# Attention's result added to the residual by VectorE instead of by GpSimd

## The chip, the cores and the metric

The kernel runs on all 8 cores of one Trainium2 chip. Each core computes one of the batch's eight sequences, with all weights of its own, and the cores exchange nothing. The time is the device time of the slowest core in microseconds (us). Engines are called as the profile calls them: PE is TensorE (matrix products), PEld its weight loads, DVE is VectorE, ACT is ScalarE, POOL is GpSimd, SP is SyncE, which here only issues DMAs.

## The reference

x has 8 sequences of 2048 tokens with 1024 features. One layer is computed, first attention, then an FFN, each behind a layer norm and each added to its input:

```python
x = x + _L0_attn_ref(_layernorm(x, axis=-1), W_query, W_key, W_value)
x = x + _L0_ffn_ref(_layernorm(x, axis=-1), w1, conv_w, conv_b, w2)
```

Attention is causal, with 16 heads of 64 features and no projection behind it: softmax(q k / 8) v goes straight into the residual. In the FFN the weights are rounded to -1, 0 or 1 times a scale that is their mean absolute value, the activations are rounded to 8 bits with a scale per token, and between the two products stand a depthwise convolution of width 3 over the tokens and SiLU.

## The kernel before, in words

**Stages.** The program has a stretch for the first norm, the values and the first queries and keys (to about 131 us), attention (131 to about 535 us), a turn between the two (the last quarter of x1 goes to DRAM and comes back tile by tile) and the FFN (from about 574 us). `attention_over` (L298) lets every engine wait until attention is over.

**Attention.** Heads go in 8 pairs (`hp`), queries in 4 tiles of 512 (`t`), keys in chunks of 128. One pair has 4 + 8 + 12 + 16 = 40 units (`unit_of`, L35); a unit is the scores of both heads of the pair for 512 queries and 128 keys. Every engine's program runs over the same slots, one per unit, and what is done in which slot is written out by hand:
- PE (L733): in each slot the scores of the unit into psS (two buffers), in four of ten slots half a projection of the next pair's queries or keys, and then the products with the values, `context(u)` (L690), of units some slots back. They sum up in psPV, of which there is one for both heads. So the first product of a tile waits for v_epi, that is, until the tile before it has been read. The units on the diagonal wait for g_mask.
- ACT (L926): the exponential of each unit, psS to PT.
- DVE (L1200): in slot 3 of ten the cast of the next pair's queries, in slot 8 that of its keys, some small operations that bound the exponent (`norm_max`, `norm_product`, `place_bias`), the weights' steps (`weight_step`, L1131), and at slots 7, 15, 27 and 43 of a pair (the last is slot 3 of the next) `normalize_ctx` (L1109), for tiles 0 to 3.
- POOL (L503): the masks of diagonal units (L464), squares of queries and keys (L455), loads and casts of the projection weights, and at slots 8, 16, 28 and 44 `add_ctx` (L468). In the last pair, `spill_x1` (L480) sends a finished quarter of x1 to DRAM right behind.

**The tile's end before.** `normalize_ctx` takes the reciprocals of the softmax sums (L1117, 8 columns), waits until GpSimd is through with the buffer of two tiles ago (g_x1), and multiplies the two heads' 4 x 64 columns of psPV by them into the buffer `ctx` (L1125, two operations of 256 columns). Then v_epi lets PE use psPV again. `add_ctx` on GpSimd waits for v_epi and adds `ctx` to x1 in four operations of 128 columns (L475).

**The weights' steps.** Beside attention VectorE goes through the FFN's weights, 32 pieces of 1 MB: in pairs 0 to 3 it sums their absolute values (L1136), in pairs 4 to 7 it rounds them in three operations (L1145, L1148, L1151). SP loads a piece (L335), and from pair 4 on stores the rounded one (L363); step i waits until the store of step i - 2 has landed.

**In the FFN** DVE's `taps` (L1297) is an operation of the same form as the new ones: a PSUM tile times a scalar per partition plus an SBUF tile, in place, 256 columns. `add_out` (L1359) is the same with 512.

Of the kernel before, what the change touches and what calls it, by code (L numbers as in the profile page):

```python
# [7 lines left out]
F32 = mybir.dt.float32  # L8
# [4 lines left out]
ALU = mybir.AluOpType  # L13
# [3 lines left out]
D = 1024  # L17
H = 16
DH = 64
# [8 lines left out]
NP = 8  # L28
# [6 lines left out]
def unit_of(u):  # L35

    hp, s = divmod(u, UN)
    t = 3 if s >= 24 else 2 if s >= 12 else 1 if s >= 4 else 0
    return hp, t, s - FIRST[t]
# [14 lines left out]
def build_program():  # L54
# [23 lines left out]
    with es:  # L78
        def sem(name):
            return es.enter_context(nc.semaphore(name))  # L80

        def sb(name, shape, dt, at=es):
            return at.enter_context(nc.sbuf_tensor(name, shape, dt))

        def ps(name, shape, dt, at=es):
            return at.enter_context(nc.psum_tensor(name, shape, dt))
# [41 lines left out]
        g_mask = sem("g_mask")  # L128
        t_pv = sem("t_pv")
        v_epi = sem("v_epi")  # L130
        g_x1 = sem("g_x1")

        v_ws = sem("v_ws")
        v_fin = sem("v_fin")
# [45 lines left out]
        x1 = sb("x1", [128, NT * D], F32, esA)  # L180
# [15 lines left out]
        recb = sb("recb", [128, 8], F32, esA)  # L196
# [8 lines left out]
        esA1.close()  # L205
        esA2 = ExitStack()
        PT = sb("PT", [128, RP * 1024], BF16, esA2)
        ctx = sb("ctx", [128, 2 * 512], F32, esA2)
        psS = [ps(f"psS{i}", [128, 1024], F32, esA2) for i in range(2)]
        psPV = ps("psPV", [128, 1024], F32, esA2)  # L210
        esA2.close()
# [86 lines left out]
        def attention_over(e):  # L298
            e.wait_ge(t_pv, NU)
            e.wait_ge(v_epi, 4 * NP)  # L300
            e.wait_ge(g_x1, 4 * NP)
            e.wait_ge(a_exp, NU)
            e.wait_ge(v_ws, NSTEP)
            e.wait_ge(v_fin, 6)
            e.wait_ge(d_x1s, 16 * 4)
            e.wait_ge(d_wo[0], 16 * 16)
            e.wait_ge(d_wo[1], 16 * 16)
# [125 lines left out]
        def _(e):  # L433
# [6 lines left out]
            def cast_wqk(hp, w):  # L440

                if hp >= 2:
                    e.wait_ge(t_qk, 8 * (hp - 1))
                e.wait_ge(d_wqk, 16 * (2 * hp + w + 1))
                at = ((hp % 2) * 2 + w) * D
                e.tensor_copy(wqkb[:, at:at + 512], wqkst[:, 0:512])
                e.tensor_copy(wqkb[:, at + 512:at + 1024],
                              wqkst[:, 512:1024]).then_inc(g_wqk, 1)

            def square(c, w):  # L450
                if c >= 1:
                    e.wait_ge(t_nrm, c)
                e.wait_ge(v_qk, 2 * c + w + 1)
                src = (q_chunk, k_chunk)[w](c)
                e.tensor_tensor(sqb[:, 512 * w:512 * (w + 1)], src, src,  # L455
                                ALU.mult).then_inc(g_sq, 1)

            def mask_unit(u):
                hp, t, kc = unit_of(u)
                j = kc - 4 * t  # L460
                e.wait_ge(a_exp, u + 1)
                sl = pt_unit(u).rearrange("p (h w) -> p h w", w=512)[
                    :, :, 128 * j:128 * (j + 1)]
                e.tensor_tensor(sl, sl,  # L464
                                maskt[:].unsqueeze(1).to_broadcast([128, 2, 128]),
                                ALU.mult).then_inc(g_mask, 1)

            def add_ctx(hp, t):  # L468
                it = 4 * hp + t
                e.wait_ge(v_epi, it + 1)  # L470
                xsl = x1[:, 4 * t * D:(4 * t + 4) * D].rearrange(
                    "p (m d) -> p m d", d=D)
                for m in range(4):
                    xm = xsl[:, m, 128 * hp:128 * (hp + 1)]
                    inst = e.tensor_tensor(  # L475
                        xm, xm, ctx[:, 512 * (it % 2) + 128 * m:
                                    512 * (it % 2) + 128 * (m + 1)], ALU.add)
                inst.then_inc(g_x1, 1)

            def spill_x1(t):  # L480
                e.wait_ge(g_x1, 4 * (NP - 1) + t + 1)
                e.dma_start(
                    out=x1scr[512 * t:512 * (t + 1), :]
                    .rearrange("(m p) d -> p m d", p=128),
                    in_=x1[:, 4 * t * D:(4 * t + 4) * D].rearrange(
                        "p (m d) -> p m d", d=D)).then_inc(d_x1s, 16)
# [16 lines left out]
            for slot in range(NU + 8):  # L503
                hp, s = divmod(slot, UN)
                if 1 <= slot <= NU:
                    php, pt, pkc = unit_of(slot - 1)
                    if pkc >= 4 * pt:
                        mask_unit(slot - 1)
                if hp < NP - 1 and s in (3, 13, 23, 33):
                    square(4 * (hp + 1) + s // 10, 0)  # L510
                if hp < NP - 1 and s in (9, 19, 29, 39):
                    square(4 * (hp + 1) + s // 10, 1)
                for t in range(4):
                    if s == (8, 16, 28, 4)[t]:
                        if t < 3 and hp < NP:
                            add_ctx(hp, t)
                        if t == 3 and hp >= 1:
                            add_ctx(hp - 1, 3)
                        if t < 3 and hp == NP - 1:
                            spill_x1(t)  # L520
                        if t == 3 and hp == NP:
                            spill_x1(3)
                if hp < NP - 2 and s == 5:
                    cast_wqk(hp + 2, 0)
                    load_wqk(hp + 2, 1)
                if hp < NP - 2 and s == 18:
                    cast_wqk(hp + 2, 1)
                    if hp + 3 < NP:
                        load_wqk(hp + 3, 0)
# [488 lines left out]
        def _(e):  # L1018
            own = 0

            def done(inst):

                nonlocal own
                inst.then_inc(v_own, 1)
                own += 1
# [80 lines left out]
                e.tensor_scalar(nbias[:, c % 8:c % 8 + 1], cbc[:, 1:2], -0.125,  # L1106
                                -80.0, ALU.mult, ALU.max).then_inc(v_bias, 1)

            def normalize_ctx(it):  # L1109
                hp, t = divmod(it, 4)  # L1110
                last = UN * hp + FIRST[t] + 4 * t + 3
                pv = psPV[:].rearrange("p (h w) -> p h w", w=512)[
                    :, :, 0:4 * VW].rearrange("p h (m v) -> p h m v", v=VW)
                e.wait_ge(t_pv, last + 1)
                if it >= 1:
                    e.wait_ge(v_epi, it)
                done(e.reciprocal(recb[:].rearrange("p (h m) -> p h m", m=4),  # L1117
                                  pv[:, :, :, DH]))
                settled()
                if it >= 2:  # L1120
                    e.wait_ge(g_x1, it - 1)
                cx = ctx[:, 512 * (it % 2):512 * (it % 2 + 1)].rearrange(
                    "p (m h d) -> p h m d", h=2, d=DH)
                for h in range(2):
                    inst = e.tensor_tensor(  # L1125
                        cx[:, h], pv[:, h, :, 0:DH],
                        recb[:, 4 * h:4 * h + 4].unsqueeze(2).to_broadcast(
                            [128, 4, DH]), ALU.mult)
                inst.then_inc(v_epi, 1)

            def weight_step(k):  # L1131
# [68 lines left out]
            for slot in range(NU + 8):  # L1200
                hp, s = divmod(slot, UN)
                if hp < NP - 1 and s % 10 == 3:
                    place_qk(4 * (hp + 1) + s // 10, 0, psQK)
                if hp < NP - 1 and s % 10 == 8:
                    place_qk(4 * (hp + 1) + s // 10, 1, psQK)
                if s == 7 and hp < NP:
                    normalize_ctx(4 * hp)
                if s == 15:
                    normalize_ctx(4 * hp + 1)
                if s == 27:  # L1210
                    normalize_ctx(4 * hp + 2)
                if s == 3 and hp >= 1:
                    normalize_ctx(4 * hp - 1)
                c = 4 * (hp + 1) + s // 10 - 1
                if c < 4 * NP and hp < NP:
                    if s % 10 == 3:
                        norm_max(c)
                    if s % 10 == 7:
                        norm_product(c)
                if hp < NP and s % 10 == 1 and 3 <= c - 1 < 4 * NP:  # L1220
                    place_bias(c - 1)
                if hp < NP and s in STEPS:
                    weight_step(8 * hp + STEPS[s])
                if (hp, s) in ((2, 8), (4, 8)):
                    sum_columns(hp // 2 - 1)
                if (hp, s) in ((2, 10), (4, 10)):
                    mean_weight(hp // 2 - 1)
                if (hp, s) in ((2, 11), (4, 11)):
                    place_scale(hp // 2 - 1)
# [228 lines left out]
```

## Time and profile before

| | |
|---|---|
| median of 3 runs | 1125.39 us (1122.07 to 1125.64) |
| the profiled execution | 1124.14 us |
| its slowest core (core 1), first to last instruction | 1122.6 us |
| all cores | 1113.4 to 1122.6 us |
| PE busy | 910.1 us (81%), 7340 instructions |
| DVE busy | 800.9 us (71%), 1293 |
| ACT busy | 697.0 us (62%), 1100 |
| POOL busy | 678.5 us (60%), 908 |
| the products in `normalize_ctx` (L1125) | 64, of 420 ns |
| the sums in `add_ctx` (L475) | 128, of 601 ns |

The profiled execution's own time is 1.5 us more than the span of its slowest core. A busy share is a mean over stages with different limits, so the stages have to be read one by one. Times in the rows are counted from the first instruction of the core.

### The profile page before, as it was taken

To read this page: it belongs to the slowest core of one execution; us is meant where nothing else is said; L and a number is where in the kernel's file an instruction comes from. 1 tells how busy PE (TensorE), PEld (TensorE's weight loads), DVE (VectorE), ACT (ScalarE), POOL (GpSimd) and SP (SyncE) were. 2 spreads that over 40 slices of the span, in tenths; PEclk is the share of its full clock that TensorE was granted. 3 is DMA by queue.
4 is the path that set the end of the run, shared out by engine and by line. 5 is a ranking of instruction groups with operands and counts; after the bars stand their busy time and mean duration, and the time that the engine had idled before them with its cause. 6 is when DMAs were issued, how large, how long until landed. Compare 5 with 4: busy or idle time off the path is not lost.

```text
span 1122.6 us, 23912 instructions; the slowest of 8 cores (1113.4 to 1122.6 us)
## 1 busy us (share of the span) xinstructions
PE 910.1 (81%) x7340; PEld 542.6 (48%) x7340; DVE 800.9 (71%) x1293; ACT 697.0 (62%) x1100; POOL 678.5 (60%) x908
## 2 busy tenths in 40 slices
PE   1599899999988797873057668898989999999898
PEld 0244355555544353432045546565656566666443
DVE  3364367677678978864447888989898988887731
ACT  2443388888867586774078776766767675766300
POOL 2100357576576757552034497796959598998680
PEclk9899999999989899966577988999999999999899
DMA  8830066565666656698573331242333333333111
GB/s 249 271 106 1 19 241 213 208 223 205 213 191 212 202 176 208 194 286 271 196 258 101 112 113 57 76 151 91 137 113 133 113 116 111 107 106 109 39 38 75
DMA packets 39468, 169.50 MB, mean 151 GB/s; under 512 B 4913, under 2 KB 5042, under 8 KB 30642
## 3 DMA queue, kind: packets, MB, share of 16 engines
q1 hardware_dynamic: 34930, 151.21, 40.2%
q0 software_dynamic: 4416, 16.78, 4.7%
q8 instruction: 63, 1.03, 0.4%
q14 instruction: 59, 0.48, 0.1%
HBM read 142.80 MB, written 25.17 MB: 150 GB/s over the span
## 4 chain that ended last, share of the span: by engine, by line
PE 41%; DVE 19%; issue 11%; DMA 10%; POOL 9%; ACT 9%; SPq 1%; DVEq 1%; POOLq 0%; ACTq 0%
PE psO L800 10%; PE psM L782 9%; PE psQK L625 6%; POOL hs L565 5%; DMA t2scr<-t8s 5%; PE psS L682 4%; PE psV L608 4%; PE psPV L701 4%; DVE hs L1297 3%; DVE amx L1316 2%; ACT PT L902 2%; ACT hs L963 2%; DVE t1s L1145 2%; ACT tb L967 2%; DVE lnc L1242 1%
## 5 line engine op out<-in xcount | busy, mean ns | idle before, releaser
L902 ACT ACTIVATE PT<-psS,nbias 128x1024 bf16<-128x1024 f32 (+1 forms) x320 | 297.4, 987 | 77.9 <-PE psS L682 73.9
L782 PE MATMUL psM<-xqT,w1b 128*128 128x258 bf16 x2048 | 252.2, 284 | 38.1 <-DVE hs L1297 36.8
L556 POOL TENSOR_TENSOR hs<-hs,tb 128x256 f32<-128x256 f32 x256 | 199.9, 810 | 108.0 <-DVE hs L1297 103.8
L782 PEld LDWEIGHTS psM<-xqT,w1b 128*128 128x128 fp8e4 x2048 | 205.1, 101 | 86.4 <-issue 47.7
L963 ACT ACTIVATE hs<-psM,convb_s,convw_s 128x256 f32<-128x256 f32 x256 | 146.7, 573 | 92.3 <-PE psM L782 83.4
L565 POOL TENSOR_TENSOR hs<-hs,srow 128x256 f32<-128x256 f32 x256 | 189.9, 775 | 11.6 <-ACT srow L981 11.6
L701 PE MATMUL psPV<-vaug,PT 128*128 128x65 bf16 x2176 | 117.3, 201 | 31.1 <-DVE ctx L1125 17.6
L682 PE MATMUL psS<-qT,kT 64*128 64x512 bf16 (+3 forms) x640 | 120.0, 372 | 24.7 <-ACT PT L902 22.1
L701 PEld LDWEIGHTS psPV<-vaug,PT 128*128 128x128 bf16 x2176 | 93.9, 102 | 92.3 <-issue 72.5
L625 PE MATMUL psQK<-ln1T,wqkb 128*128 128x512 bf16 x480 | 130.3, 397 | 3.4 <-DVE qT L1071 2.3
L464 POOL TENSOR_TENSOR PT<-PT,mask_s 128x256 bf16<-128x256 bf16 x128 | 93.1, 742 | 57.2 <-ACT PT L902 55.7
L1297 DVE SCALAR_TENSOR_TENSOR hs<-psM,convw_s,hs 128x256 f32<-128x256 f32 x256 | 108.3, 474 | 23.8 <-ACT tb L967 23.1
L967 ACT ACTIVATE tb<-psM,convw_s 128x256 f32<-128x256 f32 x256 | 121.7, 475 | 0.0
L800 PE MATMUL psO<-w2T,hqa 128*128 128x512 fp8e4 x512 | 117.2, 384 | 0.0
L800 PE MATMUL psO<-w2T,hqb 128*128 128x512 fp8e4 x512 | 114.7, 379 | 2.4 <-DVE hqb L1347 1.7
L475 POOL TENSOR_TENSOR x<-x,ctx 128x128 f32<-128x128 f32 x128 | 72.9, 601 | 72.3 <-DVE ctx L1125 72.1
L1316 DVE TENSOR_REDUCE amx<-hs 128x256 f32<-128x1024 f32 x56 | 108.6, 1940 | 4.6 <-ACT hs L974 4.6
L455 POOL TENSOR_TENSOR sqb<-qT 128x512 bf16<-128x512 bf16 x32 | 34.2, 1070 | 92.2 <-DVE qT L1071 91.8
L800 PEld LDWEIGHTS psO<-w2T,hqa 128*128 128x128 f16 x512 | 50.6, 99 | 57.2 <-issue 3.1
L800 PEld LDWEIGHTS psO<-w2T,hqb 128*128 128x128 f16 x512 | 49.8, 98 | 58.6 <-issue 3.3
L974 ACT ACTIVATE hs<-hs 128x1024 f32<-128x1024 f32 x64 | 68.2, 1065 | 10.6 <-POOL hs L556 10.5
L1136 DVE TENSOR_REDUCE smalls<-wbuf 128x1 f32<-128x2048 f32 x32 | 72.7, 2273 | 0.0
(116 smaller groups left out, 1066.2 us busy)
## 6 DMA issues: line engine op xcount, KB each, us to landing
wbuf<-w1q SPq DMA_DIRECT2D x32, 1024.0 KB, 5.6
wbuf<-w2p SPq DMA_DIRECT2D x32, 1024.0 KB, 6.4
w1b<-t1scr SPq DMA_DIRECT2D x64, 512.0 KB, 3.6
x<-x SPq DMA_DIRECT2D x16, 512.0 KB, 16.1
wqkst<-wqk POOLq DMA_DIRECT2D x16, 512.0 KB, 5.8
x1scr<-x POOLq DMA_DIRECT2D x4, 2048.0 KB, 13.5
x1t<-x1scr SPq DMA_DIRECT2D x16, 512.0 KB, 4.8
x1g<-x1scr SPq DMA_DIRECT2D x16, 512.0 KB, 4.7
```

Of the source, the lines that this page charges most:

```text
L556: e.tensor_tensor(hs_quad(q)[:, part], hs_quad(q)[:, part], tb_quad(q)[:, part], ALU.add).then_inc(g_add, 1)
L565: inst = e.tensor_tensor(part, part, srow[:, at:at + GRP], ALU.mult)
L625: inst = e.matmul(bank[:], wqkb[:, at:at + 128], ln1T[:, x0:x0 + 512], start=(kc == 0), stop=(kc == 7))
L682: inst = e.matmul(bP[:, 512 * h + 128 * j:512 * (h + 1)], kT[64 * h:64 * (h + 1), k0:k0 + 128], qT[64 * h:64 * (h + 1), q0:q0 + n], start= ...
L701: inst = e.matmul(psPV[:, 512 * h + VW * m:512 * h + VW * (m + 1)], pt_unit(u)[:, p0:p0 + 128], vaug[:, v0:v0 + VW], start=(kc == 0 and m ...
L782: inst = e.matmul(psM[j][:, 0:GRP + 2], w1b[:, at:at + 128], xqT[:, x0:x0 + GRP + 2], start=(kc == 0), stop=(kc == 7))
L800: inst = e.matmul(psO[n][:], hq_of(g)[:, at:at + 128], w2T[:, D * kc + 512 * n: D * kc + 512 * (n + 1)], start=(kc == 0), stop=(kc == 31))
L902: e.activation(out=pt_unit(u).rearrange("p (h w) -> p h w", w=512)[:, :, 128 * j:512], in_=psS[u % 2][:].rearrange("p (h w) -> p h w", w=512)[
L963: e.activation(out=hs_quad(q)[:, GRP * j:GRP * (j + 1)], in_=psM[j][:, 2:GRP + 2], func=AF.Identity, scale=convw[:, 3 * hh + 2:3 * hh + 3] ...
L967: e.activation(out=tb_quad(q)[:, GRP * j:GRP * (j + 1)], in_=psM[j][:, 0:GRP], func=AF.Identity, scale=convw[:, 3 * hh:3 * hh + 1]).then_i ...
L1297: e.scalar_tensor_tensor(sl, psM[j][:, 1:GRP + 1], convw[:, 3 * hh + 1:3 * hh + 2], sl, ALU.mult, ALU.add).then_inc(v_tap, 1)
L1316: done(e.tensor_reduce(amx[:], rows, AX.X, ALU.max, apply_absolute_value=True))
```

## The change

`ctx`, the semaphore g_x1 and all waits on it go. `normalize_ctx` becomes `add_ctx` on DVE, in the same slots: reciprocals as before, and then, for each of 4 groups of 128 queries and each of 2 heads, one operation of 64 columns that multiplies psPV by the reciprocal of its partition, adds x1 and writes x1. That is 8 operations for 2, and 256 in all for 64. GpSimd's `add_ctx` goes, 128 operations. v_epi now tells also that x1 is finished, and the spills wait for it.

```diff
-            def add_ctx(hp, t):
-                it = 4 * hp + t
-                e.wait_ge(v_epi, it + 1)
-                xsl = x1[:, 4 * t * D:(4 * t + 4) * D].rearrange(
-                    "p (m d) -> p m d", d=D)
-                for m in range(4):
-                    xm = xsl[:, m, 128 * hp:128 * (hp + 1)]
-                    inst = e.tensor_tensor(
-                        xm, xm, ctx[:, 512 * (it % 2) + 128 * m:
-                                    512 * (it % 2) + 128 * (m + 1)], ALU.add)
-                inst.then_inc(g_x1, 1)
-
             def spill_x1(t):
-                e.wait_ge(g_x1, 4 * (NP - 1) + t + 1)
+                e.wait_ge(v_epi, 4 * (NP - 1) + t + 1)
...
-            def normalize_ctx(it):
+            def add_ctx(it):
                 hp, t = divmod(it, 4)
...
                 settled()
-                if it >= 2:
-                    e.wait_ge(g_x1, it - 1)
-                cx = ctx[:, 512 * (it % 2):512 * (it % 2 + 1)].rearrange(
-                    "p (m h d) -> p h m d", h=2, d=DH)
-                for h in range(2):
-                    inst = e.tensor_tensor(
-                        cx[:, h], pv[:, h, :, 0:DH],
-                        recb[:, 4 * h:4 * h + 4].unsqueeze(2).to_broadcast(
-                            [128, 4, DH]), ALU.mult)
+                for m in range(4):
+                    x0 = (4 * t + m) * D + 128 * hp
+                    for h in range(2):
+                        xsl = x1[:, x0 + DH * h:x0 + DH * (h + 1)]
+                        inst = e.scalar_tensor_tensor(
+                            xsl, pv[:, h, m, 0:DH],
+                            recb[:, 4 * h + m:4 * h + m + 1], xsl, ALU.mult,
+                            ALU.add)
                 inst.then_inc(v_epi, 1)
```

## Rows read from the trace of the kernel before

**Rows 1.** Busy time in three stretches: length, engines (instructions), PEclk, DMA, GB/s.
```profile
131.00:306.60 175.60, 164.25 (x1850) 90.05 (x1850) 125.56 (x206) 152.47 (x190) 110.41 (x178) 1.00 0.60 208
306.60:446.00 139.40, 114.71 (x1158) 60.42 (x1159) 114.73 (x176) 96.08 (x121) 98.97 (x118) 0.91 0.62 197
446.00:537.00 91.00, 56.94 (x620) 31.69 (x618) 59.62 (x79) 56.74 (x69) 43.49 (x56) 0.73 0.78 244
```
**Rows 2.** PE's longest wait, 131 to 306.6 us: us in total, times, longest.
```profile
PE psS L682 <- ACT PT L902: 9.4, 20, 0.6
```
**Rows 3.** PE's waits, 306.6 to 537 us (two) and in pair 6 (last).
```profile
PE psPV L701 <- DVE ctx L1125: 17.6, 11, 6.0
PE psPV L701 <- POOL PT L464: 12.9, 14, 2.0
...
PE psPV L701 <- POOL PT L464: 1.9, 2, 1.0
```
**Rows 4.** Chain of waits, 448 to 537 us: shares by line, one piece.
```profile
by line: DMA t2scr<-t8s 62.8%; DVE t8s L1151 10.2%; DVE t1s L1145 9.9%; DVE t1s L1148 8.4%; issue 5.0%; SPq L335 2.2%; POOL x L475 1.9%; DVE ctx L1125 0.6%; DVEq L1028 0.3%; DVE recb L1117 0.2%; DVEq L1144 0.1%; SPq L329 0.1%; SPq L358 0.1%
...
484.77 3.34 DVE t1s L1148
```
**Rows 5.** DVE's groups with shapes: busy us, mean ns | idle before.
```profile
L1297 DVE SCALAR_TENSOR_TENSOR hs<-psM,convw_s,hs 128x256 f32<-128x256 f32 x256 | 108.3, 474 | 23.8 <-ACT tb L967 23.1
...
L1125 DVE TENSOR_TENSOR ctx<-psPV,recb 128x256 f32<-128x256 f32 x64 | 24.3, 420 | 5.4 <-DVE recb L1117 5.2
L1359 DVE SCALAR_TENSOR_TENSOR x1g<-psO,amc,x1g 128x512 f32<-128x512 f32 x32 | 23.7, 742 | 26.0 <-PE psO L800 26.0
```
**Rows 6.** DVE in order of time in the FFN: start, us.
```profile
652.42 1.65 DVE L1297 SCALAR_TENSOR_TENSOR hs<-psM,convw_s,hs 128x256 f32<-128x256 f32 x4
```
**Rows 7.** DVE in order of time in attention: start, us.
```profile
267.17 0.76 DVE L1125 TENSOR_TENSOR ctx<-psPV,recb 128x256 f32<-128x256 f32 x2 [0.17 <-DVE recb L1117]
...
268.10 0.65 DVE L1084 TENSOR_TENSOR nmx<-nmx 128x1 f32<-128x1 f32 x1
...
271.31 0.76 DVE L1125 TENSOR_TENSOR ctx<-psPV,recb 128x256 f32<-128x256 f32 x2 [0.17 <-DVE recb L1117]
...
375.90 5.78 DVE L1148 TENSOR_SCALAR t1s<-t1s 128x2048 f16<-128x2048 f16 x1
...
534.24 0.76 DVE L1125 TENSOR_TENSOR ctx<-psPV,recb 128x256 f32<-128x256 f32 x2 [0.17 <-DVE recb L1117]
```
**Rows 8.** PE in order of time, at the change to pair 3.
```profile
268.41 0.59 PE L701 MATMUL psPV<-vaug,PT 128*128 128x65 bf16 x14
...
272.31 0.67 PE L701 MATMUL psPV<-vaug,PT 128*128 128x65 bf16 x16
```
**Rows 9.** PE in order of time, pair 4; waits in brackets.
```profile
317.47 0.68 PE L701 MATMUL psPV<-vaug,PT 128*128 128x65 bf16 x16 [1.31 <-DVE ctx L1125]
...
323.63 0.40 PE L701 MATMUL psPV<-vaug,PT 128*128 128x65 bf16 x8 [1.75 <-POOL PT L464]
```
**Rows 10.** PE in order of time on core 3, pair 5.
```profile
382.63 0.60 PE L701 MATMUL psPV<-vaug,PT 128*128 128x65 bf16 x8 [3.27 <-POOL PT L464]
```
**Rows 11.** POOL in order of time, pair 5, tile 0's end.
```profile
375.94 1.68 POOL L475 TENSOR_TENSOR x<-x,ctx 128x128 f32<-128x128 f32 x4
...
379.21 1.91 POOL L464 TENSOR_TENSOR PT<-PT,mask_s 128x256 bf16<-128x256 bf16 x3
```
**Rows 12.** L1148's instructions: shortest, median, longest in ns.
```profile
L1148 DVE TENSOR_SCALAR t1s<-t1s x32: 694/754/5778, 314.1 to 531.9; 128x2048 f16<-128x2048 f16 x32
```
**Rows 13.** DVE's groups on core 3: busy us, mean ns.
```profile
L1148 DVE TENSOR_SCALAR t1s<-t1s 128x2048 f16<-128x2048 f16 x32 | 26.7, 835 | 3.4
```
**Rows 14.** POOL in order of time at attention's end.
```profile
535.14 1.68 POOL L475 TENSOR_TENSOR x<-x,ctx 128x128 f32<-128x128 f32 x4 [9.07 <-DVE ctx L1125]
```
**Rows 15.** Spans and mean granted clock of the cores: core 3.
```profile
core 3: 1122.1 us, clock 0.921
```
**Rows 16.** Busy time from 318.0 to 321.4 us, columns as rows 1.
```profile
318.00:321.40 3.40, 3.40 (x27) 1.99 (x24) 3.19 (x5) 1.00 (x3) 3.12 (x4) 0.50 0.87 321
```

More of the change, by code:

```diff
@@ L130, in build_program @@
         v_epi = sem("v_epi")
-        g_x1 = sem("g_x1")
         v_ws = sem("v_ws")
@@ L207, in build_program @@
         PT = sb("PT", [128, RP * 1024], BF16, esA2)
-        ctx = sb("ctx", [128, 2 * 512], F32, esA2)
         psS = [ps(f"psS{i}", [128, 1024], F32, esA2) for i in range(2)]
@@ L300, in attention_over @@
             e.wait_ge(v_epi, 4 * NP)
-            e.wait_ge(g_x1, 4 * NP)
             e.wait_ge(a_exp, NU)
@@ L514, in _ @@
                     if s == (8, 16, 28, 4)[t]:
[L515 to L518, printed above, removed]
                         if t < 3 and hp == NP - 1:
@@ L1206, in _ @@
                 if s == 7 and hp < NP:
-                    normalize_ctx(4 * hp)
+                    add_ctx(4 * hp)
                 if s == 15:
-                    normalize_ctx(4 * hp + 1)
+                    add_ctx(4 * hp + 1)
                 if s == 27:
-                    normalize_ctx(4 * hp + 2)
+                    add_ctx(4 * hp + 2)
                 if s == 3 and hp >= 1:
-                    normalize_ctx(4 * hp - 1)
+                    add_ctx(4 * hp - 1)
                 c = 4 * (hp + 1) + s // 10 - 1
```

## The prediction

> **What bounds the kernel now.** I read the windows by stage first. While attention runs and the weights' mean is being summed (131 to 306.6 us) TensorE is busy 164.25 of 175.60 us at a granted clock of 1.00; from 306.6 to 446 VectorE is busy 114.73 of 139.40 us and TensorE 114.71 at a clock of 0.91; from 446 to 537 neither is full [rows 1]. TensorE's waits say why. In the first stretch its largest wait is 9.4 us for the exponentials, and none is for VectorE's context product [rows 2]. After 306.6 it waits 17.6 us for that product and 12.9 us for GpSimd's masks [rows 3]. From 448 on, the chain of waits is 62.8% the store of rounded weights, and an operation of VectorE stretched to 3.34 us lies on it [rows 4]. So there are three stretches: TensorE with VectorE just in time; VectorE and TensorE waiting for each other in turn; and the weights' chain through DMA, in which the attention work has room until its last tile.
>
> **The price of the new operations.** A tile (a head pair and 512 queries) loses two products of 256 columns and gets eight operations of 64 columns that read PSUM, a pointer scalar and x1. The same form stands in the FFN: 474 ns at 256 columns, 742 ns at 512 [rows 5], so (742 - 474) / 256 = 1.05 ns per column and 474 - 192 x 1.05 = 273 ns for 64 columns. Four of 256 columns in a row take 1.65 us [rows 6], so one starts every (1.65 - 0.47) / 3 = 0.393 us, and at 64 columns every 0.393 - 0.201 = 0.192 us. A tile: 7 x 0.192 + 0.273 = 1.62 us, against 0.76 us for the pair [rows 7]: **0.86 us more**, of VectorE's time and of the delay until PSUM is released. From below: the old product starts again after 0.76 - 0.42 = 0.34 us [rows 5, 7]; at 64 columns that would be 0.14, the block 7 x 0.14 + 0.27 = 1.25 us (0.49 more). From above, without any overlap, 8 x 0.273 = 2.18 us (1.42 more). I take 0.86, since it comes from the same form of operation; the lower end would take 0.37 from each of the 19 tiles counted below, 7.0 us.
>
> The Trainium skill ("VectorE: DVE Perf Modes", section "The DRAIN you can't avoid") says that the next operation does not start before the pipe of the one in front is empty. By that rule the block would be the 2.18 us. The rows speak against it, since four operations of 474 ns fit into 1.65 us.
>
> **Up to 306.6 us.** psPV is single: the next tile's first product waits for v_epi. A release takes 0.14 us (products end at 534.24 + 0.76 = 535.00, GpSimd starts at 535.14) [rows 7, 14]. Tile 3: products end at 267.93, TensorE uses psPV at 268.41, room 0.34 after the release. Tile 0 of the next pair: end 272.07, use 272.31, room 0.10 [rows 7, 8]. Between tiles 3 and 0 VectorE runs without a gap, so tile 0 is late by both excesses; but its one-column comparison, which took 0.65 us beside GpSimd's adds [rows 7] and by the slope above (0.273 - 64 x 0.00105) needs about 0.2, gives 0.4 back. TensorE loses 2 x 0.86 - 0.4 - 0.10 = 1.2 us at each of three changes of pair: **+3.6 us**. Tiles 1 and 2 I cost at nothing: before them TensorE still has scores and a projection to issue between two uses of psPV, and what queues behind their products on VectorE (the norm product, the cast of kT, for which GpSimd's square and the next projection wait) is followed by a wait for TensorE's next projection. If that cover were gone, each would cost up to 0.86.
>
> **306.6 to 446 us.** Here TensorE waits at nearly every tile (1.31 us at 317.47) [rows 9]; eleven tiles give 11 x 0.86 = 9.5, less the first one's room, 9.1. Against it:
> - The comparison at three changes of pair: -1.2.
> - GpSimd's queue. It now stands in its four adds until v_epi and for 1.7 us [rows 11], and cast, weight load, squares and four masks queue behind. The mask of tile 1's first diagonal unit comes late: TensorE waits 1.75 us at 323.63 [rows 9]. Without the adds the exponential releases it long before. Core 1: -1.75 in pair 4 and two such waits in pair 6, 1.9 together [rows 3]. Core 3 waits 3.27 us in pair 5 [rows 10]; in pair 4 I take the 1.75 of core 1.
> - A rounding operation of VectorE took 5.78 us at 375.90 [rows 7], where the shortest takes 0.69 [rows 12]; GpSimd worked through from 375.94, beginning with its adds [rows 11]. Without them the masks run earlier and spread out: -5.1 on core 1 (it covers pair 5's mask wait). Core 3's 32 operations of this kind took 26.7 us together, 32 x 0.69 = 22.1 and no such stall among them [rows 13].
> - Smaller stretches of VectorE's weight operations beside the adds: an estimate of 0.1 per tile, -1.2, since a median rounding operation is 0.06 over the shortest [rows 12] and a tile's adds meet one or two; bounds nothing and twice that.
>
> Core 1: 9.1 - 1.2 - 1.75 - 1.9 - 5.1 - 1.2 = **-2.0 us**; core 3: 9.1 - 1.2 - 1.75 - 3.3 - 1.2 = **+1.6 us**.
>
> **From 446 us.** Only tile 2 of pair 6 (0.86) and the very last tile (0.86) are on the chain; the others fall into waits for the stores. If those waits went, tiles at 0.86 each would come back. At the end GpSimd's adds, 1.68 us with 0.14 to release them [rows 14], are gone from before the spill. The 3.34 us operation [rows 4] is 2.65 over its floor; I give it back by half on core 1 (-1.3), not on core 3. Core 1: 0.86 + 0.86 - 1.82 - 1.3 = **-1.4**; core 3: **-0.1**. The first three spills leave 1 us earlier and share the same queues: nothing. The buffer's place is used by nothing else, and the wait on g_x1 was for sums long done: nothing. In the FFN no instruction changes.
>
> **Sum.** Core 1: 3.6 - 2.0 - 1.4 = +0.2; core 3: 3.6 + 1.6 - 0.1 = +5.1. Core 1 is the slowest at 1122.6 us, core 3 stands at 1122.1 [rows 15]. Which cores have the long stalls may differ between executions, so I take the middle, +2.6. The profiled execution is 1124.14 us, 1.5 over its span and 1.25 under the median; the change is the same against either: 1125.39 + 2.6 = **1128.0 us**.
>
> **The rivals.** *Slower, by the clock.* After the 1.31 us wait the granted clock is 0.50, the lower level of 1.2 GHz, from 318.0 to 321.4 [rows 9, 16]. The new waits at the three changes of pair before 306.6 are about 0.5 and 0.7 us each, in a stretch at 1.00 throughout. If they cost the clock as that one did, each gives 3.4 us at half speed, 1.7 us: 3 x 1.7 = 5.1 more, 1133.1 us. For it: the cause is the same kind of wait. Against it: waits of up to 0.6 us there left the clock alone. [...]
>
> *Slower still:* no overlap between the short operations; (1.42 - 0.86) x 19 tiles = 10.6 more (19: six before 306.6, eleven, two), 1138.6 us. It is against [rows 6].
>
> *Faster, by the port.* VectorE and GpSimd hinder each other more widely than I count: both stretched operations go whole (another -1.3), the smaller stretches give 2.0, not 1.2 (-0.8), and with stalls gone the clock does not fall twice between 306.6 and 446 (-3.4): 0.2 - 5.5 = -5.3 on core 1, 1120.1 us. For it: [rows 7, 11]. Against it: masks and squares remain, a large part of that stall lay beside masks [rows 11], and core 3 ended as late without it.
> The Trainium skill ("SBUF — State Buffer", "SBUF: two separate sides") calls the port pair of VectorE and GpSimd an exclusive lock, held for a whole instruction, with the loser blocked. The trace agrees in kind: 5.78 us for 0.69. The new operation's form ran at a mean of 474 ns beside a busy GpSimd [rows 5], so it seems not to ask for the lock.
>
> *Nothing:* the excess falls into waits everywhere; 1125.4 us. [rows 8] leave too little room for it.
>
> **Chances.** A measurement can tell about 0.3% (3.4 us) from no change. Forecast with its own range of 1123 to 1133: 0.45, of which 0.27 lies within 0.3% and 0.18 above. Clock: 0.17. No overlap: 0.04. Port: 0.28, all below. Nothing: 0.06. So faster 0.28, same 0.33, slower 0.39. The range of 1119 to 1136 takes in the clock and most of the port case, and also holds the lower end of the new operations' price (1121.0); it leaves out no overlap and the tails.
>
> **What would show it.** The new operation's mean near 273 ns and eight within 1.6 us; TensorE waiting for VectorE before 306.6 at each change of pair, in sum 3 to 5 us, with the clock at 1.00 or below it there; its wait for masks after 306.6 falling from 12.9 to about 7 us and that for v_epi rising from 17.6 to about 25; no rounding operation over 3 us; the last spill issued about 0.6 us after the last product. The forecast is wrong if the new operations don't overlap, if the clock falls in the first stretch, or if the stalls stay although the adds are gone.

## The result, and the profile after

The changed kernel took 1133.43 us (median of 4 runs, 1130.9 to 1134.83) against 1124.72 us before (1122.07 to 1125.64): ratio 1.0077, 95% interval 1.0061 to 1.0094. It is slower by 8.7 us where 2.6 were forecast. That is inside the range and on the forecast's side of no change, but 5.4 us above the forecast's own number (1128.0) and just above its own range of 1123 to 1133. It is at the number of the rival "slower, by the clock" (1133.1). The medians here and below are over all executions of a kernel; a few of these ran 1 to 7% longer, with part of the chip at a lower clock, and the ratios leave those out. The kernel before ran again beside each group of experiments (1124.0 to 1125.2 us), and their ratios are against that.

The windows by stage on the slowest core, core 5, cut at the same points of the work as [rows 1] (its attention starts at 135.7 us; columns are length, PE, PEld, DVE, ACT, POOL, PEclk, DMA, GB/s):

```profile
135.70:316.70 181.00, 166.43 (x1850) 90.62 (x1850) 138.92 (x296) 152.63 (x190) 85.68 (x118) 0.99 0.60 202
316.70:458.00 141.30, 119.03 (x1149) 61.59 (x1150) 119.06 (x241) 95.89 (x121) 73.80 (x74) 0.86 0.62 199
458.00:549.00 91.00, 57.96 (x630) 31.97 (x627) 61.38 (x116) 57.82 (x69) 31.25 (x31) 0.73 0.75 236
```

Pairs 0 to 3 take 181.0 instead of 175.6 us, and the granted clock there is no longer 1.00. In the next stretch it is 0.86 instead of 0.91. VectorE is busier in the first stretch by 13 us, GpSimd less busy by 25.

TensorE's waits on the same core, 131 to 310 us and 310 to 540 us (total, times, longest), to be held against [rows 2] and [rows 3]:

```profile
PE psS L663 <- ACT PT L883: 9.0, 19, 0.6
PE psPV L682 <- DVE x L1105: 1.9, 4, 0.6
PE psPV L682 <- POOL PT L461: 1.2, 3, 0.4
```
```profile
PE psPV L682 <- DVE x L1105: 25.5, 13, 5.0
PE psS L663 <- ACT PT L883: 11.2, 30, 0.8
PE psPV L682 <- POOL PT L461: 7.0, 10, 1.2
```

After 310 us the wait for v_epi went from 17.6 to 25.5 us and that for masks from 12.9 to 7.0. Before 310 us there are new waits at psPV at each change of pair, 3.1 us in sum with what is put down to masks. VectorE at the end of pair 4's tile 0, and then TensorE at the change to pair 3 and behind that same tile 0, in order of time:

```profile
323.18 1.63 DVE L1125 TENSOR_SCALAR t1s<-wbuf,smalls 128x2048 f16<-128x2048 f32 x1
...
326.85 0.20 DVE L1098 RECIPROCAL recb<-psPV 128x8 f32<-128x8 f32 x1
327.51 1.63 DVE L1105 SCALAR_TENSOR_TENSOR x<-psPV,recb,x 128x64 f32<-128x64 f32 x8 [0.46 <-DVE recb L1098]
```
```profile
277.65 0.59 PE L682 MATMUL psPV<-vaug,PT 128*128 128x65 bf16 x14 [0.40 <-POOL PT L461]
...
282.23 0.65 PE L682 MATMUL psPV<-vaug,PT 128*128 128x65 bf16 x16 [0.63 <-DVE x L1105]
...
329.28 0.93 PE L682 MATMUL psPV<-vaug,PT 128*128 128x65 bf16 x14 [2.48 <-DVE x L1105]
```

Eight operations take 1.63 us, as worked out. Where [rows 9] had 1.31 us of waiting, 2.48 stand now. The wait of 0.40 at 277.65 is put down to a mask, but it is the first product of a tile, the operations of tile 3 ended 0.26 us before it, and in the kernel before the product at this place ([rows 8], 268.41) started while that mask was still running (268.07 to 268.74).

The new operations and the rounding ones among VectorE's groups, and the latter's shortest, median and longest:

```profile
L1105 DVE SCALAR_TENSOR_TENSOR x<-psPV,recb,x 128x64 f32<-128x64 f32 x256 | 52.1, 276 | 3.8 <-DVE recb L1098 0.5
...
L1128 DVE TENSOR_SCALAR t1s<-t1s 128x2048 f16<-128x2048 f16 x32 | 29.6, 925 | 3.8 <-DVE t1s L1125 0.5
```
```profile
L1128 DVE TENSOR_SCALAR t1s<-t1s x32: 693/696/1343, 324.9 to 544.6; 128x2048 f16<-128x2048 f16 x32
```

And the clock, in windows with columns as [rows 1]: during the fall in pair 2 and just before it, and at the one in pair 4:

```profile
236.70:240.10 3.40, 3.40 (x33) 2.23 (x32) 2.36 (x4) 1.25 (x3) 2.08 (x3) 0.50 0.38 128
233.30:236.70 3.40, 2.05 (x25) 1.20 (x24) 3.29 (x13) 2.62 (x5) 0.88 (x2) 1.00 0.91 337
```
```profile
329.00:345.90 16.90, 15.97 (x101) 7.88 (x102) 13.05 (x30) 7.21 (x10) 9.58 (x8) 0.50 0.55 168
```

TensorE was busy 2.05 of 3.40 us while three waits fell together at the change to pair 2 (0.46 us for an exponential, 0.63 for the new operations, 0.22 for a norm; the kernel before has only the first of them there), and then had half the clock (1.2 GHz) for 3.4 us. In pair 4, after the wait of 2.48 us, it had 1.2 GHz for 16.9 us.

The Trainium skill ("TensorE: Matmul & The Clock Gate", Part 1) says that a clock gate lowers the array's clock to 1.2 GHz after idling and restores it after work. The rows agree on the level; but what stood before the fall in pair 2 was no idle engine, only short waits within work.

**All cores.** One core's span is one of eight, so here is the mean over the cores of each profiled execution, in us. Pairs 0 to 3 run from the first score to the reciprocals of tile 3 of pair 3, pairs 4 to 6 to those of tile 3 of pair 6, pair 7 to the last reciprocals, the spill until x1's last quarter has landed. "Rest" is from there to the last instruction; the stretch before the first score (131.6 to 132.9 us) is left out. "Low" is time at the lower granted clock, "v_epi" and "masks" are TensorE's waits at psPV in pairs 4 to 6. Each row is one execution. The expectations of the first four experiments count the stages from the first score to the first score of pair 4 (before: 175.7 and 160.3); the order is the same.

| kernel | pairs 0-3 | pairs 4-6 | pair 7 | spill | rest | low 0-3 | low 4-6 | v_epi | masks |
|---|---|---|---|---|---|---|---|---|---|
| before | 179.7 | 161.8 | 58.7 | 11.3 | 574.7 | 0.0 | 24.6 | 8.3 | 8.9 |
| after | 185.4 | 166.8 | 58.6 | 10.2 | 575.3 | 4.3 | 36.3 | 15.2 | 5.3 |
| e1_nosum | 178.3 | 152.3 | 57.3 | 9.3 | 574.2 | 0.0 | 14.4 | 7.2 | 5.3 |
| e2_split | 185.4 | 174.9 | 59.8 | 12.0 | 575.2 | 2.6 | 43.3 | 15.0 | 6.3 |
| e3_early | 183.1 | 161.6 | 59.0 | 10.2 | 575.3 | 6.4 | 23.3 | 10.8 | 4.8 |
| e4_fill | 184.7 | 162.3 | 57.9 | 10.2 | 575.1 | 1.7 | 25.1 | 10.2 | 5.8 |
| e5_early2 | 178.9 | 155.6 | 54.8 | 10.0 | 575.3 | 0.0 | 15.6 | 10.3 | 4.8 |
| e6_steps | 182.8 | 169.2 | 59.5 | 10.0 | 575.4 | 0.4 | 39.3 | 5.5 | 6.2 |
| e7_both | 178.9 | 163.4 | 58.6 | 10.3 | 575.5 | 0.0 | 29.5 | 3.0 | 6.1 |
| e8_fillbefore | 179.7 | 161.2 | 58.9 | 11.4 | 575.6 | 0.0 | 20.1 | 3.7 | 11.8 |
| e9_late | 185.7 | 166.4 | 58.2 | 10.1 | 575.2 | 4.7 | 32.2 | 16.8 | 4.6 |
| e10_fill5 | 179.7 | 155.6 | 55.0 | 10.2 | 575.0 | 0.0 | 13.7 | 6.3 | 4.4 |

The change cost 5.7 us in pairs 0 to 3 and 5.0 in pairs 4 to 6, and gave 1.1 at the spill.

### The profile page after: what moved, and what is told of

The parts are those of the page before. It is cut to its first block, busy times and chain, and to the rows that moved or that the text cites. A ratio compares the mean times of both kernels' runs of the same rounds, so it can differ in the third digit from the quotient of the medians.

```text
span 1133.4 us, 23909 instructions; the slowest of 8 cores (1122.4 to 1133.4 us)
## 1 busy us (share of the span) xinstructions
PE 920.1 (81%) x7340; PEld 545.3 (48%) x7340; DVE 820.4 (72%) x1485; ACT 698.1 (62%) x1100; POOL 616.4 (54%) x780
## 4 chain that ended last, share of the span: by engine, by line
PE 43%; DVE 20%; issue 10%; DMA 10%; ACT 8%; POOL 7%; SPq 1%; DVEq 1%; POOLq 0%; ACTq 0%
PE psM L763 11%; PE psO L781 10%; PE psQK L606 7%; POOL hs L546 5%; PE psV L589 4%; PE psS L663 4%; PE psPV L682 4%; DMA t2scr<-t8s 4%; DVE hs L1277 3%; DVE x L1105 3%; ACT hs L944 2%; DVE t1s L1125 2%; DVE amx L1296 2%; ACT tb L948 2%; ACT PT L883 2%
## 5 line engine op out<-in xcount | busy, mean ns | idle before, releaser
L546 POOL TENSOR_TENSOR hs<-hs,srow 128x256 f32<-128x256 f32 x256 | 189.8, 774 | 11.4 <-ACT srow L962 11.4
L461 POOL TENSOR_TENSOR PT<-PT,mask_s 128x256 bf16<-128x256 bf16 x128 | 100.5, 798 | 100.7 <-ACT PT L883 99.1
L663 PE MATMUL psS<-qT,kT 64*128 64x512 bf16 (+3 forms) x640 | 123.1, 382 | 22.7 <-ACT PT L883 20.2
L1277 DVE SCALAR_TENSOR_TENSOR hs<-psM,convw_s,hs 128x256 f32<-128x256 f32 x256 | 108.4, 474 | 25.0 <-ACT tb L948 24.6
L452 POOL TENSOR_TENSOR sqb<-kT 128x512 bf16<-128x512 bf16 x32 | 39.8, 1245 | 73.4 <-DVE kT L1052 73.4
L781 PEld LDWEIGHTS psO<-w2T,hqb 128*128 128x128 f16 x512 | 49.8, 98 | 58.6 <-issue 3.3
```

Of the source, the lines that this page charges most:

```text
L546: inst = e.tensor_tensor(part, part, srow[:, at:at + GRP], ALU.mult)
L663: inst = e.matmul(bP[:, 512 * h + 128 * j:512 * (h + 1)], kT[64 * h:64 * (h + 1), k0:k0 + 128], qT[64 * h:64 * (h + 1), q0:q0 + n], start= ...
L781: inst = e.matmul(psO[n][:], hq_of(g)[:, at:at + 128], w2T[:, D * kc + 512 * n: D * kc + 512 * (n + 1)], start=(kc == 0), stop=(kc == 31))
L1277: e.scalar_tensor_tensor(sl, psM[j][:, 1:GRP + 1], convw[:, 3 * hh + 1:3 * hh + 2], sl, ALU.mult, ALU.add).then_inc(v_tap, 1)
```

## The experiments

**What goes and what comes, each alone.** e1_nosum is the kernel before without GpSimd's sums (x1 lacks attention's result); e2_split is the kernel before with the products cut up.

```diff
 e1_nosum
-                        if t < 3 and hp < NP:
-                            add_ctx(hp, t)
-                        if t == 3 and hp >= 1:
-                            add_ctx(hp - 1, 3)
...
-                e.wait_ge(g_x1, 4 * (NP - 1) + t + 1)
+                e.wait_ge(v_epi, 4 * (NP - 1) + t + 1)
```

> The kernel before without GpSimd's sums: the two products of 256 columns stay on VectorE and write ctx, which nobody reads; attention's result is left out of x1. This is what the change removes, without what it adds. Theory A (the sums hinder masks and VectorE's rounding after pair 3, and the added cost of eight operations outweighs that): pairs 0 to 3 take 175.6 us as before, pairs 4 to 6 take 154 to 157 us instead of 160.3 (mean over the cores), the spill behind the last tile 1.8 us less, in all 4 to 8 us faster than before, 1117 to 1121 us. Rival B (the relief is worth nothing, since another wait ends last at the same place): pairs 4 to 6 stay at 160 us and only the 1.8 us at the end are gained, 1123 us.

```diff
 e2_split
-                for h in range(2):
-                    inst = e.tensor_tensor(
-                        cx[:, h], pv[:, h, :, 0:DH],
...
+                for m in range(4):
+                    for h in range(2):
+                        inst = e.tensor_scalar(
+                            cx[:, h, m], pv[:, h, m, 0:DH],
+                            recb[:, 4 * h + m:4 * h + m + 1], None,
+                            ALU.mult)
```

> The kernel before, with the products cut into eight operations of 64 columns (PSUM times a scalar per partition, written to ctx); GpSimd's sums stay. This is what the change adds, without what it removes. Theory A: pairs 0 to 3 as long as after the change or a little shorter (179 to 181 us instead of 175.6), pairs 4 to 6 at 168 to 173 us, longer than after the change (165.4) because the sums still stand in GpSimd's queue; 1134 to 1142 us. Rival B (relief worth nothing): pairs 4 to 6 as after the change, 165 us, total about 1133 plus the 1.8 us of the last sums, 1135 us. Rival C (the loss comes from reading x1 and PSUM in one operation, not from the number of operations): within 3 us of the kernel before.

e1_nosum took 1111.32 us, ratio 0.9888 (0.9845 to 0.9931), by the ratio 12.6 us less than before (7.8 to 17.4). e2_split took 1147.44 us, ratio 1.0199 (1.0168 to 1.0230), 22.4 more (18.9 to 25.9). Both fall outside the ranges of theory A, which had each effect smaller. Their sum, +9.8 us, is the change's +8.7 within these intervals, which are too wide to exclude that the two parts act on each other by a few us. Rival B falls (9.5 us go in pairs 4 to 6 without the sums), and so does rival C: these operations do not read x1, they take 276 ns all the same, and the loss is there:

```profile
L1126 DVE TENSOR_SCALAR ctx<-psPV,recb 128x64 f32<-128x64 f32 x256 | 52.0, 276 | 6.2 <-DVE recb L1117 6.0
```

The relief is not where I had put it. Without the sums the rounding operations still take 987 ns, mean over the cores (963 after the change, 924 before), so GpSimd's masks and squares stretch them as before. What fell in pairs 4 to 6 is the wait for masks, by 3.6 us, that for v_epi, by 1.1, and the time at the lower clock, from 24.6 to 14.4 us. In pairs 0 to 3 1.4 us were gained. A wait for a mask of 0.4 us that went is part of it; the rest is not traced.

**The same work on VectorE, with an early release.** e3_early keeps the two products, gives v_epi at once, and adds ctx to x1 later, on VectorE, in one operation of 512 columns.

```diff
 e3_early
+            def add_ctx(it):
+                hp, t = divmod(it, 4)
...
+                e.wait_ge(v_epi, it + 1)
+                e.tensor_tensor(
+                    xsl, xsl, ctx[:, 512 * (it % 2):512 * (it % 2 + 1)]
+                    .rearrange("p (m w) -> p m w", w=128),
+                    ALU.add).then_inc(v_x1, 1)
...
+                if s == 8 and hp >= 1:
+                    add_ctx(4 * hp - 1)
+                if s in (10, 16, 28) and hp < NP:
+                    add_ctx(4 * hp + (10, 16, 28).index(s))
```

> VectorE does both, but apart: the two products of 256 columns into ctx, v_epi at once, and one addition of 512 columns to x1 at slots 8, 10, 16 and 28, behind other work; nothing on GpSimd. VectorE's time per tile rises by about 0.6 us (after the change: 0.86), the release of psPV is as early as before. Theory A (the loss is the late release of psPV at tiles without room): pairs 0 to 3 within 1 us of 175.6, pairs 4 to 6 at 156 to 163 us, total 1118 to 1126 us. Rival D (the loss is VectorE's occupancy, wherever it stands): about two thirds of the change's loss, pairs 0 to 3 at 179 us, pairs 4 to 6 at 164 us, total 1130 us.

1131.12 us, ratio 1.0050 (1.0036 to 1.0065): the number of rival D, though pairs 4 to 6 (161.6 us) came as theory A had them and pairs 0 to 3 (183.1) are longer than either had. TensorE's waits on core 7 show why in pairs 0 to 3, and again (4.5 us) behind:

```profile
PE psN L651 <- DVE nrm L1162: 2.5, 1, 2.5
```

This is the weights' mean of pairs 2 and 4, which VectorE reached late because two additions stood in front of it; the clock fell behind it (6.4 us low in pairs 0 to 3). So e3_early does not separate the two; e5_early2 has the additions elsewhere.

```diff
 e5_early2, against e3_early
-                if s == 8 and hp >= 1:
-                    add_ctx(4 * hp - 1)
-                if s in (10, 16, 28) and hp < NP:
...
                     place_scale(hp // 2 - 1)
+                if 1 <= hp and s == (11 if hp < NP else 4):
+                    add_ctx(4 * hp - 1)
+                if s in (12, 21, 31) and hp < NP:
+                    add_ctx(4 * hp + (12, 21, 31).index(s))
```

> As e3_early (products, v_epi, and later one addition of 512 columns, all on VectorE), but the additions stand at slots 11, 12, 21 and 31, behind the weights' mean of pairs 2 and 4 and behind casts. In e3_early TensorE waited 2.5 us in pair 2 and 4.4 us in pair 4 for that mean (psN from nrm), because two additions stood in front of it. Theory A': with them out of the way pairs 0 to 3 take what they take without GpSimd's sums (178.3 us by the reciprocal of tile 3 of pair 3; e3_early 183.1, the changed kernel 185.4), pairs 4 to 6 155 to 160 us (e3_early 161.6), total 1116 to 1124 us. Rival D (VectorE's occupancy): pairs 0 to 3 at 180 us or more, total 1127 us or more.

1115.93 us, ratio 0.9921 (0.9907 to 0.9936): **faster than both kernels**, by the ratio 8.9 us under the kernel before, and just below the range of theory A'. Pairs 0 to 3 (178.9 us) and 4 to 6 (155.6) are as that theory had them. Its counterpart e9_late has the same operations, but the addition right behind the products and v_epi behind it:

```diff
 e9_late, in normalize_ctx
                             [128, 4, DH]), ALU.mult)
-                inst.then_inc(v_epi, 1)
+                done(inst)
+                settled()
...
+                e.tensor_tensor(
+                    xsl, xsl, ctx[:, 512 * (it % 2):512 * (it % 2 + 1)]
+                    .rearrange("p (m w) -> p m w", w=128),
+                    ALU.add).then_inc(v_epi, 1)
```

> The operations of e5_early2 (two products of 256 columns into ctx, one addition of 512 columns to x1, all on VectorE), but the addition stands right behind the products and v_epi is given only behind it, as in the changed kernel. VectorE's operations are the same as in e5_early2; the release of psPV is later by the addition of about 0.7 us and the wait for ctx to be written, 0.9 us in all (the changed kernel: about 0.8 later than before). Theory A (the late release is the loss): as the changed kernel or slightly slower, 1131 to 1138 us, pairs 0 to 3 at 184 to 187 us, pairs 4 to 6 at 165 to 170 us. Rival D (VectorE's time, wherever it stands): as e5_early2, 1113 to 1119 us. In between: both count.

1135.13 us, ratio 1.0098 (1.0077 to 1.0119), as theory A had it. VectorE's groups in e5_early2 and in e9_late:

```profile
L1120 DVE TENSOR_TENSOR x<-x,ctx 128x512 f32<-128x512 f32 x32 | 26.6, 849 | 0.1
L1109 DVE TENSOR_TENSOR ctx<-psPV,recb 128x256 f32<-128x256 f32 x64 | 24.2, 420 | 5.4 <-DVE recb L1101 5.2
```
```profile
L1105 DVE TENSOR_TENSOR ctx<-psPV,recb 128x256 f32<-128x256 f32 x64 | 24.2, 420 | 3.8 <-DVE recb L1099 0.7
L1113 DVE TENSOR_TENSOR x<-x,ctx 128x512 f32<-128x512 f32 x32 | 23.3, 730 | 3.3
```

VectorE is busy 50.8 us with them in the faster kernel and 47.5 in the slower one, and 52.1 with its 256 operations in the changed kernel. So its busy time is not what cost 19 us. The two in order of time at a change of pair, e5_early2 and then e9_late, VectorE and TensorE:

```profile
273.65 0.76 DVE L1109 TENSOR_TENSOR ctx<-psPV,recb 128x256 f32<-128x256 f32 x2 [0.17 <-DVE recb L1101]
```
```profile
274.66 0.67 PE L685 MATMUL psPV<-vaug,PT 128*128 128x65 bf16 x16
```
```profile
278.89 0.76 DVE L1105 TENSOR_TENSOR ctx<-psPV,recb 128x256 f32<-128x256 f32 x2
279.75 0.69 DVE L1113 TENSOR_TENSOR x<-x,ctx 128x512 f32<-128x512 f32 x1
```
```profile
280.59 0.65 PE L683 MATMUL psPV<-vaug,PT 128*128 128x65 bf16 x16 [0.56 <-DVE x L1113]
```

In the first, TensorE does not wait; in the second it waits 0.56 us for the end of the addition. The 0.79 us from 279.65 to 280.44 are not in front of it in the first.

The two kernels differ in one thing more: in e9_late the addition also stands earlier in VectorE's queue, in front of casts and norms. That is not what cost the time. From e5_early2 to e9_late TensorE's waits in pairs 4 to 6 for the casts of queries and keys and for norms fell, from 3.2 to 1.7 us (mean over the cores), while those for v_epi rose from 10.3 to 16.8 and the time at the lower clock from 15.6 to 32.2.

**The clock.** e4_fill lets TensorE repeat the scores of some units of the changed kernel, into the same PSUM tile and with the same result, where it would wait soon after.

```diff
 e4_fill and e8_fillbefore
+AGAIN = ({5: 1, 9: 1}, {9: 2, 17: 4, 29: 3})
...
-                for h in range(2):
+                more = (AGAIN[hp // 4].get(u % UN, 0)
+                        if 0 < u // UN < 7 else 0)
+                for h in list(range(2)) * (1 + more):
```

> The changed kernel; TensorE issues the scores of a few units again (once at slots 5 and 9 of pairs 1 to 3; twice at slot 9, four times at slot 17, three times at slot 29 of pairs 4 to 6), same operands and same result, which fills part of the time in which it would wait for v_epi. Theory A with the clock as a part of the loss (the granted clock is at its lower level for 3.4 us or more in pairs 0 to 3 on six of eight cores and for 35 us in pairs 4 to 6, where it was 0 and 24 us before): low time falls to 0 in pairs 0 to 3 and by 10 us or more in pairs 4 to 6, total 1126 to 1131 us. Rival E (the lower clock falls into waits and costs nothing, or the repeated scores cost what the clock gives back): within 2 us of the changed kernel's 1133.4, or above.

1128.79 us, ratio 1.0039 (1.0024 to 1.0054): 4.6 us less than the changed kernel (4.3 by the ratios), with more work on TensorE. Low time in pairs 4 to 6 fell from 36.3 to 25.1 us, in pairs 0 to 3 from 4.3 to 1.7 (to 0 was expected). The repeated scores compute nothing that is used, so about half of the change's loss goes back to the clock. That they also moved the order in which later work falls is not excluded.

> The kernel before, with TensorE's scores repeated at the same places as in e4_fill. In the kernel before the granted clock is at its lower level for 24.6 us of pairs 4 to 6 (mean over the cores). If repeated scores give back the clock lost in waits for v_epi, it gains 1 to 3 us here too, less than the 4.6 us by which e4_fill was faster than the changed kernel, since its waits for v_epi are half as long: 1121 to 1124 us. Rival E: the repeated scores delay the exponentials and cost more than the clock gives back: 1126 us or more.

The same in the kernel before: 1124.75 us, ratio 0.9996 (0.9986 to 1.0006), no change. Low time fell by 4.5 us, but the wait for masks rose from 8.9 to 11.8 us. The gain of 1 to 3 us did not come, and the loss of rival E neither. Less time at the lower clock is thus not a gain by itself.

> e5_early2 with the repeated scores of e4_fill. Granted clock at its lower level in pairs 4 to 6: 15.6 us in e5_early2 (mean over the cores), 36.3 in the changed kernel, 24.6 before. Where the waits for v_epi are short again, the repeated scores should have little to give back: 1113 to 1119 us, within the interval of e5_early2; if the clock's loss is still there to be had, 1110 to 1113 us.

On top of e5_early2: 1112.74 us, ratio 0.9909 (0.9888 to 0.9930). The interval overlaps that of e5_early2, and the means over the cores, 1107.0 and 1107.1 us, do not differ. Whether it gains is open.

**The steps in front of the reciprocal.** e6_steps is the changed kernel, e7_both is e5_early2, both with the weights' steps moved.

```diff
 e6_steps and e7_both
+        LATER = {8: 0, 9: 1, 16: 2, 19: 3, 28: 4, 29: 5, 34: 6, 39: 7}
...
-                if hp < NP and s in STEPS:
-                    weight_step(8 * hp + STEPS[s])
+                at = STEPS if hp in (2, 4) else LATER
+                if hp < NP and s in at:
+                    weight_step(8 * hp + at[s])
```

> The changed kernel with the weights' steps moved behind the tile ends in pairs 0, 1, 3, 5, 6 and 7: slots 8, 9, 16, 19, 28, 29, 34, 39 instead of 4, 9, 14, 19, 24, 29, 34, 39. The reciprocals of tiles 0 to 2 no longer stand behind a step of 2.3 or 3.6 us; VectorE's work is the same. Theory A (delay of v_epi at tiles without room): the waits of TensorE for v_epi in pairs 0 to 6 fall from 17.6 us to 9 or less, total 1122 to 1129 us. Rival D (VectorE is simply full in pairs 4 to 6): pairs 4 to 6 stay at 166 to 167 us, total 1131 us or more.

> e5_early2 with the steps moved as in e6_steps. If both terms (late v_epi because of the eight operations, and because of steps in front of the reciprocal) are real and separate, this is the fastest: 1112 to 1120 us, below the kernel before. Rival: the steps two by two make the casts late, and TensorE waits for qT instead; no better than e5_early2.

e6_steps took 1138.81 us, ratio 1.0125 (1.0111 to 1.0140), and e7_both 1126.26 us, ratio 1.0009 (0.9999 to 1.0019), slower than e5_early2. The wait for v_epi did fall, to a third (15.2 to 5.5 us, and 10.3 to 3.0), and pairs 0 to 3 of e6_steps gained 2.6 us. But in pairs 4 to 6 two rounding steps in a row hold up the casts, as e7_both's rival had it: TensorE's waits for the casts rose from 0.5 to 8.8 us in e6_steps and from 1.2 to 10.1 in e7_both (mean over the cores). TensorE's waits in e6_steps on core 4, from 310 to 480 us:

```profile
PE psQK L607 <- DVE qT L1053: 7.8, 5, 2.0
...
PE psPV L683 <- DVE x L1106: 5.3, 4, 2.5
```

Both expected totals (1122 to 1129 and 1112 to 1120) were misses: I had priced the wait taken away, not the one that took its place. Rival D had e6_steps' total (1131 or more), but not for its reason: VectorE's work did not change, and pairs 4 to 6 grew from 166.8 to 169.2 us.

## Why the prediction was right, and where it was not

- **The price of the new operations: right.** 273 ns were forecast, 276 measured; the block 1.62 and 1.63 us. Starts overlapped, as in [rows 6]. The Trainium skill's rule that the next operation waits for an empty pipe ("VectorE: DVE Perf Modes", "The DRAIN you can't avoid") would give 2.18 us, and the rows do not bear it out. The same section adds that a next operation that is not held starts earlier, and 1.63 us for eight operations of 276 ns agrees with that.
- **Pairs 0 to 3: the mechanism right, the clock left to a rival.** Forecast +3.6 us. On cores 3 and 6, where the clock held, it is +4.5 and +4.4. The mean is +5.7, with 4.3 us at half clock, which make about 4.3 / 2 = 2.1 us. By its own sign ("if the clock falls in the first stretch") the forecast was wrong here: the clock fell on six of eight cores. One reading was wrong too. The comparison of 0.65 us at 268.10 stood beside a mask of GpSimd (268.07 to 268.74), not beside the adds, which began at 268.70. After the change it stands beside a cast and takes 0.41, so it gave back 0.25 and not 0.4:

```profile
268.07 0.67 POOL L464 TENSOR_TENSOR PT<-PT,mask_s 128x256 bf16<-128x256 bf16 x1
```
```profile
277.57 0.41 DVE L1065 TENSOR_TENSOR nmx<-nmx 128x1 f32<-128x1 f32 x1
```

- **Pairs 4 to 6: the failed step is the price of the late release.** For the eleven tiles up to 446 us and tile 2 of pair 6 the forecast had 9.1 + 0.86 = 10.0 us of waiting, and the clock at nothing. e2_split, which has this cost without the relief, shows 13.1 us in these pairs, with 18.7 us more at half clock (24.6 to 43.3), which make up to 9.3 us. With the relief against it, of 9.3 us in the middle of cores 1 and 3, the forecast for these pairs was +0.7 us; measured are +5.0. In the changed kernel TensorE's waits for v_epi grew by 6.9 us (8.3 to 15.2), the masks gave 3.6 back, and 11.7 us more at half clock are up to 5.9. These three come to as much as 9.2 us, so they overlap; the clock's exact share of the 5.0 stays open.
- **The relief in pairs 4 to 6: the sum right, its terms not, which is luck.** The forecast had 11.2 us on core 1 and 7.5 on core 3; e1_nosum gained 9.5. The masks came as forecast, 3.6 us. The long stall of a rounding operation went on all cores (the longest takes 1.34 us; before, six of eight cores had one of 5.78). But its term of -5.1 us was wrong: before, the two cores without it took 159.4 and 162.4 us for these pairs, and the six with it 162.1 in the mean, so in that execution it was worth about 1 us. I had no row that showed what it was worth to the end. Nor did the smaller stretches give 1.2; the rounding operations took 0.92 us before and 0.96 after, mean over the cores. In place of these terms e1_nosum has 10.2 us less at half clock.
- **From 446 us: right in sum.** Forecast -1.4 and -0.1; measured -0.1 for pair 7 (from -2.5 to +1.7 on single cores) and -1.1 at the spill. GpSimd issues the last spill 0.54 us behind the last operation instead of behind its adds (core 5: products end at 548.50):

```profile
549.04 0.81 POOL L467 DMA_DIRECT2D x1scr<-x  x1 [9.02 <-DVE x L1105]
```

- **The rival by the clock: the number right, its place half right.** It had 3 x 1.7 = 5.1 us more in pairs 0 to 3. There it is 2.1; the rest lies in pairs 4 to 6. Its total of 1133.1 fits to 0.3 us, and that is luck in part: it stands on the same sum for pairs 4 to 6, which was 4 us short. e4_fill shows that the clock counts, by about 4.6 us.
- **The rival by the port: not borne out.** The time of rounding operations hardly moved with the sums gone (e1_nosum: 987 ns, 924 before), and in e2_split, with all sums in place and no such operation over 2.0 us, they took 813 ns, mean over the cores. The one long stall did go with the sums, but was worth little. The sums' cost was masks that came late and more time at the lower clock.
- **Cost and relief for the whole kernel.** Added up from its terms, the forecast had 15.7 us of cost (4.9, 10.0 and 0.9) and 15.5 us of relief on core 1 or 10.5 on core 3, in the middle 13.0. Each alone measured 22.4 (e2_split) and 12.6 (e1_nosum). So the miss of 6 us lies in the cost. The measured time is in the range of 1119 to 1136 because the range took in the rival by the clock, not because the forecast's sum held.

## What to carry to other kernels

Where one PSUM tile is used in turn, count first what stands between the last product of a tile and its release. Work that can follow the release should follow it, even if the engine does more in sum: two products, release and a later addition took 1115.9 us, the same operations in front of the release 1135.1. When a change lengthens or removes a wait of TensorE, price the clock with it from rows at the lower level, in every stretch where the clock already falls, not only in the one that is still at full speed. The gain is not certain: the same repeated scores gained 4.6 us in the changed kernel and nothing in the kernel before. And before a queue's step is moved out of one wait's way, look for the next wait in that queue; here the casts.

## What was not expected of the hardware

The changed kernel got faster by giving TensorE more to do. With up to four repeated scores in a slot, each pair 0.39 us long at the full clock, it took 4.6 us less, and less of pairs 4 to 6 ran at 1.2 GHz (25.1 instead of 36.3 us). And eight operations of 64 columns took as long without x1 as with it: 276 ns each in both forms, one that reads its tensor from PSUM alone (e2_split) and one with x1 as a second tensor.
